# Experts' stage as one block: gates applied before the gather, scatters that add in DRAM, two buffers each for gathered rows, results and row numbers

## The chip, the core and the metric

One core of a Trainium2 chip runs the whole program as one launch. The metric is the time of that launch on the device in microseconds (us). The core has TensorE (PE, with its weight loads shown apart as PEld), VectorE (DVE), ScalarE (ACT), GpSimd (POOL), SyncE (SP), whose queue issues most DMAs, and 16 DMA engines that all queues share. POOL issues the indirect DMAs, whose row numbers come from a table.

## The reference, cut to what matters

The program is a two-layer decoder over x of 2 x 1024 tokens with 256 features: chunked attention, cross attention, a quantised feed-forward layer, causal attention, a second cross attention, and last a mixture of experts. Only this last stage, in which each token goes to 2 of 8 experts, is touched. From the kernel's view it is:

```python
xn = layernorm(x) * gamma + beta                 # 2048 tokens x 256
probs = clip(normalised_softmax(clip(xn @ router.T)), 1e-8, 1)
gates, expert = top_k(probs, 2)                  # 2 choices per token
for each choice i of token n:
    h = silu(W_gate[e] @ (gate * xn[n])) * (W_up[e] @ (gate * xn[n]))
    y[n, i] = W_down[e] @ h                      # e = expert[n, i], 512 hidden
out = layernorm(x + (x + y[n, 0] + y[n, 1]))     # so 2 x + the two results
```

## The kernel before, in words

Tokens are handled in 16 tiles of 128 (`TILES`). `stage_experts` (L2088) runs three blocks one after the other. A block is a piece of program for each engine with a barrier of all engines at its end.

The first block routes. It normalises x into `xn` (L2308 to L2231), writes it to DRAM as `xn_rows` (L2199), multiplies it by the router, and picks two experts and two gates per token (L2328 to L2336). Each of the 4096 choices gets a slot, counted expert by expert, each expert's slots padded to whole tiles of 128; that gives 39 slot tiles (`SLOT_TILES`). TensorE turns the table round, from "slot of a choice" to "choice and gate of a slot", by 32 matmuls of one-hot matrices (`at_place`, L2378) with `tile_values` (L2278) in fp32. The results are `token` (which row to gather), `choice` (which row to scatter to), `slot_gate` and `expert`, the expert of each slot tile.

The second block is the loop over the 39 slot tiles. `lagged` (L92) writes each engine's loop as a software pipeline: in step t an engine works on tile t and on tiles t-1 and t-2 (GpSimd down to t-4). Most of it is a hardware loop over four steps a turn, the rest is unrolled ahead and behind. For a tile:

- GpSimd copies a column of `token` into `tile_token` (L2425), gathers 128 rows from `xn_rows` (L2428), and multiplies them by the gate into `row` (L2420).
- TensorE transposes `row` (L2470). ScalarE rounds it to `rows_hi` (L2503), VectorE takes the remainder `rows_lo` (L2538). In the same way the expert's weights are split into `w_hi` (ScalarE, L2493) and `w_lo` (VectorE, L2528).
- TensorE does 12 matmuls for gate and up (L2463). ScalarE applies silu (L2498), VectorE multiplies into `hidden` (L2535). TensorE transposes it (L2453), VectorE copies that to `hidden_tr` (L2522), and TensorE does 4 down matmuls, shown as 8 rows (L2476).
- ScalarE copies the result to `rows_out` (L2508), the single buffer, which it may do only when the scatter of the tile before has landed (`need(act, scattered, 16 * u2)`). GpSimd copies a column of `choice` (L2433) and scatters 128 rows to `choice_rows` (L2436), in which each token has two rows.

The third block ends the stage: SP loads both rows of each token from `choice_rows` (L2602) in 8 groups of two tiles, GpSimd adds them (L2562), VectorE adds 2 x (L2575) and takes mean and variance (L2578 to L2584), GpSimd makes the scale and offset (L2554, L2557), ScalarE normalises (L2592), and SP writes the output (L2606).

Engines run their own instructions in the written order and wait only on semaphores. Four lines matter below: `pool.wait_ge(scattered, 16 * SLOT_TILES)` ends GpSimd's loop block (L2440), `need(act, scattered, 16 * u2)` is ScalarE's (L2507), `pe.wait_ge(row_ready, t + 1)` holds the transposes of rows for GpSimd (L2467), and `pe.wait_ge(hidden_ready, u2 + 1)` holds the transposes of hidden for VectorE (L2450).

## Time and profile before

| | |
|---|---|
| median of 3 runs | 1422.87 us (1421.18 to 1423.92) |
| the profiled execution | 1422.48 us, of which the span is 1420.8 us |
| experts' stage | about 1076 to 1420.8 us of the span |
| its loop, first transposes of rows to last scatter | 1150.8 to 1380.0 us |
| busy over the span | PE 84%, DVE 62%, ACT 52%, POOL 43% |
| mean granted TensorE clock | 0.929 of 2.4 GHz |

All times within the execution are counted from the start of the span. A row of the timeline gives start, duration, engine, source line, operation, what it writes and reads, how many were merged into the row, and in brackets how long the engine was idle before it and what released it. "<-issue" means that nothing in the profile released it. DMA rows on POOL or SPq are the issue; the transfer lands later. A row of a stretch gives busy time with the number of instructions in brackets, then the granted clock (1.00 is 2.4 GHz, 0.50 is 1.2 GHz).

### The profile page before, as it was taken

The numbers are of one execution on the slowest core, as the hardware profiler recorded it, in microseconds if no ns is written. First come the engines' busy times: TensorE is split into PE (matmuls) and PEld (weight loads), VectorE is DVE, ScalarE is ACT, GpSimd is POOL, SyncE is SP. The second block draws the span as 40 slices with busy tenths as digits, with TensorE's granted clock in tenths as the row PEclk, the third lists the DMA queues.
The fourth block names the chain that finished last, engine by engine and source line by source line (L and its number), as shares of the span: only waits on it lengthen the run. The fifth ranks groups of instructions, "written<-read, shape, count | busy, mean of one in ns | idle before, by whom it ended". The sixth has DMA issues, their size and how long they took to land. (4 is left out here: it accounts for less than half of the span.)

```text
span 1420.8 us, 25057 instructions
## 1 busy us (share of the span) xinstructions
PE 1197.0 (84%) x8059; PEld 873.5 (61%) x8060; DVE 881.0 (62%) x1545; ACT 743.3 (52%) x2046; POOL 608.3 (43%) x664
## 2 busy tenths in 40 slices
PE   7888589575999999999899999998984368999970
PEld 4544367454667767776666777665763357777750
DVE  2588799773445555563445566665886656677745
ACT  2598457334556556655555566652661035555532
POOL 1155457557436223322633322101664336666635
PEclk9999799797899999999999999999996569999995
DMA  9100000010010010001010001005401001111105
GB/s 303 27 1 0 0 1 2 1 30 16 16 30 16 16 30 16 16 1 31 15 25 17 5 16 45 1 1 224 133 1 45 23 19 49 44 48 48 48 33 178
DMA packets 36136, 56.04 MB, mean 39 GB/s; under 512 B 6528, under 2 KB 27392, under 8 KB 36032
## 3 DMA queue, kind: packets, MB, share of 16 engines
q1 hardware_dynamic: 32288, 44.47, 10.5%
q0 software_dynamic: 3744, 10.23, 2.2%
q8 instruction: 59, 0.97, 0.3%
q14 instruction: 45, 0.37, 0.1%
HBM read 34.90 MB, written 9.31 MB: 31 GB/s over the span
## 5 line engine op out<-in xcount | busy, mean ns | idle before, releaser
L2016 DVE TENSOR_REDUCE ga_neg_top<-ps 128x1 f32<-128x128 f32 (+7 forms) x256 | 181.9, 752 | 195.2 <-PE ps L1786 194.8
L1897 ACT ACTIVATE ga_e<-ps,ga_neg_top 128x128 f32<-128x128 f32 (+7 forms) x256 | 188.2, 743 | 7.5 <-DVE ga_neg_top L2016 6.8
L1906 ACT COPY ga_e_tr<-ps 128x512 f32<-128x512 f32 (+3 forms) x192 | 92.0, 479 | 174.6 <-PE ps L1795 172.1
L1795 PE MATMUL ps<-ident,ga_e 128*128 128x128 f32 x1152 | 165.1, 279 | 0.8 <-DVE ga_e_tr L2024 0.8
L1811 PE MATMUL ps<-ga_e_tr,ga_v 128*64 128x256 f32 x1152 | 151.7, 391 | 4.1 <-ACT ga_att L1914 4.1
L1795 PEld LDWEIGHTS ps<-ident,ga_e 128*128 128x128 f32 x1152 | 123.3, 142 | 28.0 <-ACT ga_e L1897 14.7
L2024 DVE COPY ga_e_tr<-ps 128x128 f32<-128x128 f32 (+3 forms) x192 | 105.8, 551 | 35.1 <-PE ps L1795 34.8
L2528 DVE TENSOR_TENSOR ex_w_lo<-ex_gate_up,ex_w_hi 128x1024 fp32r<-128x1024 f32 x78 | 92.7, 1229 | 42.1 <-ACT ex_w_hi L2493 42.0
L1971 POOL TENSOR_TENSOR ga_q_lo<-shared,ga_q_hi 128x1024 fp32r<-128x1024 f32 x15 | 35.5, 2370 | 175.5 <-ACT ga_q_hi L1887 175.5
L2493 ACT CAST ex_w_hi<-ex_gate_up 128x1024 fp32r x78 | 77.9, 1046 | 50.5 <-PEq L2189 35.0
L1811 PEld LDWEIGHTS ps<-ga_e_tr,ga_v 128*64 128x64 f32 x1152 | 72.4, 136 | 48.9 <-issue 23.3
L818 POOL TENSOR_TENSOR xa_e<-xa_e,xa_recip 128x1024 f32<-128x1024 f32 x32 | 60.9, 1902 | 68.6 <-DVE xa_recip L938 68.6
L1783 PE MATMUL ps<-ga_k_hi,ga_q_hi 64*128 64x512 f32 (+3 forms) x384 | 79.2, 409 | 4.1 <-PEq L158 2.3
L493 ACT ACTIVATE ca_e<-ps,ca_neg_top 128x64 f32<-128x64 f32 x256 | 75.9, 361 | 0.2 <-DVE ca_neg_top L524 0.2
L2476 PE MATMUL ps<-ex_down,shared 128*128 x312 | 74.0, 380 | 1.8 <-DVE shared L2522 1.0
L1957 POOL TENSOR_TENSOR shared<-shared,ga_cos 128x1024 f32<-128x1024 f32 x18 | 42.6, 2368 | 75.0 <-DMA shared<-shared 71.2
L2436 POOL DMA_INDIRECT choice_rows<-shared,ex_tile_choice x39 | 59.7, 1530 | 31.9 <-POOL ex_tile_choice L2433 31.9
L1247 PE MATMUL ps<-x_tr,wide_weights 128*128 128x128 f32 x512 | 67.0, 286 | 2.0 <-ACT ga_e_tr L1906 2.0
L1247 PEld LDWEIGHTS ps<-x_tr,wide_weights 128*128 128x128 f32 x512 | 62.9, 200 | 8.2 <-issue 5.8
L1783 PE MATMUL ps<-ga_k_lo,ga_q_hi 64*128 64x512 f32 (+3 forms) x384 | 67.6, 348 | 0.0
L1783 PE MATMUL ps<-ga_k_hi,ga_q_lo 64*128 64x512 f32 (+3 forms) x384 | 67.6, 348 | 0.0
L493 ACT ACTIVATION_READ_ACCUMULATOR ca_e<-ps,ca_neg_top 128x1 f32 x256 | 65.1, 255 | 0.0
(330 smaller groups left out, 2738.7 us busy)
## 6 DMA issues: line engine op xcount, KB each, us to landing
shared<-shared SPq DMA_DIRECT2D x80, 128.0 KB, 2.4
ex_gate_up<-in_ex_gate_up SPq DMA_DIRECT2D x1, 8192.0 KB, 24.3
ex_down<-in_ex_down SPq DMA_DIRECT2D x1, 4096.0 KB, 35.7
x_tr<-in_x_tr SPq DMA_DIRECT2D x4, 512.0 KB, 7.3
x_nat<-in_x SPq DMA_DIRECT2D x1, 2048.0 KB, 11.7
xn_rows<-x_tr SPq DMA_DIRECT2D x8, 256.0 KB, 2.1
x_tr<-choice_rows SPq DMA_DIRECT2D x8, 256.0 KB, 4.9
shared<-choice_rows SPq DMA_DIRECT2D x8, 256.0 KB, 5.5
```

The source lines that it names most:

```text
L493: last = nc.scalar.activation(e[buffer][:, keys], ps_scores[buffer][:, keys], ACT.Exp, scale=SCALE, bias=neg_top[buffer][:, m:m + 1], accu ...
L1247: last = nc.tensor.matmul(bank[:, g * P:(g + 1) * P], wq[:, k, block_of], x_tr[:, k, J * P:(J + 1) * P], start=(k == 0), stop=(k == KD - 1))
L1783: nc.tensor.matmul(ps_scores(t, half)[:, k0:k1], qs[J % 2][rows, c * R + r, :], ks[slot][rows, c, 0:k1 - k0], start=(i == 0), stop=(i == 2 ...
L1795: last = nc.tensor.transpose(ps_tr[n % 2][:, (kb - k0) * P:(kb - k0 + 1) * P], e[half][t % 2][:, kb * P:(kb + 1) * P], core.ident[:])
L1811: last = nc.tensor.matmul(ps_att[half * HD:(half + 1) * HD, :], v[:, v_slot(b, kb), kv * HD:(kv + 1) * HD], e_tr[g % 2][:, kb, half, :], s ...
L1897: nc.scalar.activation(e[half][t % 2][:, 0:blocks(t) * P], ps_scores(t, half), ACT.Exp, bias=neg_top[t % 2][:, half:half + 1], accum_out=s ...
L1906: nc.scalar.copy(e_tr[g % 2][:, k0:k1, half, t % 2 * P:(t % 2 + 1) * P], ps_tr[n % 2][:, 0:(k1 - k0) * P].rearrange("p (k t) -> p k t", t= ...
L2016: nc.vector.tensor_reduce(neg_top[t % 2][:, half:half + 1], ps_scores(t, half), AX.X, ALU.max, negate=True).then_inc(top_ready, 1)
L2024: nc.vector.tensor_copy(e_tr[g % 2][:, k0:k1, half, t % 2 * P:(t % 2 + 1) * P], ps_tr[n % 2][:, 0:(k1 - k0) * P].rearrange("p (k t) -> p k ...
L2476: last = nc.tensor.matmul(core.ps_y[:, 0:D], hidden_tr[:, k, :], weights.down[:, bass.ds(y, 1), k, :].rearrange("p a n -> p (a n)"), start ...
L2493: nc.scalar.copy(w_hi[turn % 2][:, k, :], weights.gate_up[:, bass.ds(x, 1), k, :] .rearrange("p a n -> p (a n)")).then_inc(w_hi_ready, 1)
L2528: nc.vector.tensor_tensor(w_lo[turn % 2][:, k, :], weights.gate_up[:, bass.ds(x, 1), k, :].rearrange("p a n -> p (a n)"), w_hi[turn % 2][: ...
```

## The change

The three blocks become one, so both barriers inside the stage go. Within it:

- ScalarE doubles x (4 instructions, L2399 of the new file) and SP writes it to DRAM as `summed_rows`, N + 128 rows. Each scatter then adds its rows there (`compute_op=ALU.add`) instead of writing `choice_rows`. Each scatter waits for the one before to have landed, since two choices of a token go to one row. Unused slots go to the 128 spare rows.
- The gates are applied ahead of the loop: ScalarE makes two scaled copies of `xn` (32 instructions, L2412) and SP writes both to `gated_rows` (16 DMAs of 256 KB). GpSimd's multiply in the loop goes, `xn_rows` goes too, and TensorE transposes the gathered rows themselves. The first gather and ScalarE's first step wait until all of it is written.
- With no gates to carry, the routing table has two parts of bf16 (tile number and place) instead of three of fp32. VectorE now makes both parts and both one-hot halves, running sums over the experts are 3 steps instead of 8, and both choices are handled in one instruction where there were two. The `past` and `expert` instructions move behind the one-hots.
- Gathered rows, `rows_out` and the row numbers for the scatter have two buffers each. A gather waits for the transposes of the tile two before and for the gather before it; ScalarE's copy waits for the scatter two before.
- The tail loads one tensor instead of two. GpSimd's adds and VectorE's 2 x + sum go. SP waits for the scatters itself. GpSimd executes an explicit drain behind its loop, ahead of the tail's work.

```diff
-        row, tokens_in, rows_out = (flat[:, i * D + 3 * FF:(i + 1) * D + 3 * FF] for i in (1, 2, 3))
+        rows_in, rows_out = ([flat[:, i * D + 3 * FF:(i + 1) * D + 3 * FF] for i in pair] for pair in ((1, 2), (3, 4)))
         hidden_tr = flat[:, D + 2 * FF:D + 3 * FF].rearrange("p (k t) -> p k t", k=KF)
...
-        choice_rows = nc.dram_tensor("choice_rows", (2 * N + P, D), F32).ap()
+        gated_rows = nc.dram_tensor("gated_rows", (2 * N, D), F32).ap()
+
+        summed_rows = nc.dram_tensor("summed_rows", (N + P, D), F32).ap()
...
+        def fetch(pool, g, turn):
+
+            nc.gpsimd.tensor_copy(tile_source[:], column(source, g)).then_inc(source_ready, 1)
+            pool.wait_ge(source_ready, g + 1)
+            apart(pool, core.pool_waited)
+            nc.gpsimd.indirect_dma_start(rows_in[turn % 2], None, gated_rows,
+                                         bass.IndirectOffsetOnAxis(ap=tile_source[:], axis=0)).then_inc(gathered, 16)
...
+                for n in range(TILES // DOUBLED):
+                    tiles = slice(n * DOUBLED, (n + 1) * DOUBLED)
+                    sp.wait_ge(doubled_ready, n + 1)
+                    sp.dma_start(summed_rows[0:N, :].rearrange("(n p) d -> p n d", p=P)[:, tiles, :],
+                                 doubled[n // len(HALVES)][:, HALVES[n % len(HALVES)], :]).then_inc(summed_written, 16)
+                sp.dma_start(summed_rows[N:N + P, :], doubled[0][:, 0, :]).then_inc(summed_written, 16)
+                for i in range(2):
+                    for g in range(GROUPS_OF_TILES):
+                        tiles = slice(g * GROUP, (g + 1) * GROUP)
+                        sp.wait_ge(gated_ready, i * GROUPS_OF_TILES + g + 1)
+                        sp.dma_start(gated_rows[i * N:(i + 1) * N, :].rearrange("(n p) d -> p n d", p=P)[:, tiles, :],
+                                     gated[i][:, tiles, :]).then_inc(gated_written, 16)
+
+                sp.wait_ge(scattered, 16 * SLOT_TILES)
                 for g in range(GROUPS_OF_TILES):
                     tiles = slice(g * GROUP, (g + 1) * GROUP)
-                    sp.wait_ge(xn_ready, g + 1)
-                    sp.dma_start(xn_rows.rearrange("(n p) d -> p n d", p=P)[:, tiles, :], xn[:, tiles, :]).then_inc(xn_written, 16)
-
-                sp.wait_ge(xn_written, 16 * GROUPS_OF_TILES)
+                    rows = summed_rows[0:N, :].rearrange("(n p) d -> p n d", p=P)
+                    sp.dma_start(xn[:, tiles, :], rows[:, tiles, :]).then_inc(sums_loaded[g], 16)
+                for g in range(GROUPS_OF_TILES):
+                    tiles = slice(g * GROUP, (g + 1) * GROUP)
+                    sp.wait_ge(final_ready, g + 1)
+                    sp.dma_start(core.out.rearrange("(n p) d -> p n d", p=P)[:, tiles, :], xn[:, tiles, :]).then_inc(out_written, 16)
+                sp.wait_ge(out_written, 16 * GROUPS_OF_TILES)
...
-                pool.wait_ge(masks_ready, MASKS)
-                pool.wait_ge(in_tile_ready, 1)
-                for i in range(2):
-                    for part, value in enumerate((choice_iota[:, i], gate_parts[:, 0, i])):
-                        nc.gpsimd.tensor_tensor(tile_values[:, i, :, part, :], in_tile[:, i], of_tiles(value), ALU.mult).then_inc(values_ready, 1)
+                pool.wait_ge(gated_written, 16 * 2 * GROUPS_OF_TILES)
+                pool.wait_ge(sources_ready, 1)
+                fetch(pool, 0, 0)
+
+                def step(g, t, u1, u2, u3, turn):
+                    if g is not None and not at(g, 0):
+                        need(pool, rows_tr_ready, g - 1)
+                        pool.wait_ge(gathered, 16 * g)
+                        apart(pool, core.pool_waited)
+                        fetch(pool, g, turn)
+                    if u3 is not None:
+                        pool.wait_ge(down_copied, u3 + 1)
+                        apart(pool, core.pool_waited)
+                        nc.gpsimd.tensor_copy(tile_target[turn % 2][:], column(target, u3)).then_inc(target_ready, 1)
+                        pool.wait_ge(target_ready, u3 + 1)
+                        need(pool, scattered, 16 * u3)
+                        apart(pool, core.pool_waited)
+                        nc.gpsimd.indirect_dma_start(summed_rows, bass.IndirectOffsetOnAxis(ap=tile_target[turn % 2][:], axis=0),
+                                                     rows_out[turn % 2], None, compute_op=ALU.add).then_inc(scattered, 16)
+
+                pool.wait_ge(targets_ready, 1)
+                pool.wait_ge(summed_written, 16 * (TILES // DOUBLED + 1))
+                lagged(pool, SLOT_TILES, 4, step, turns=True)
+                nc.gpsimd.drain()
+
+                def finish(g):
+                    tiles = slice(g * GROUP, (g + 1) * GROUP)
+                    pool.wait_ge(var_ready, g + 1)
+                    nc.gpsimd.tensor_tensor(rstd[:, tiles], var_eps[:, tiles], core.neg_half[:].to_broadcast([P, GROUP]),
+                                            ALU.pow).then_inc(rstd_ready, 1)
+                    pool.wait_ge(rstd_ready, g + 2)
+                    nc.gpsimd.tensor_tensor(offset[:, tiles], neg_mean[:, tiles], rstd[:, tiles], ALU.mult).then_inc(offset_ready, 1)
+
+                for g in range(GROUPS_OF_TILES):
+                    finish(g)
...
-                    for t in range(TILES):
-                        last = nc.tensor.matmul(ps_slots, at_place[:, t, :], tile_values[:, i, t, :, :],
-                                                start=(i == 0 and t == 0), stop=(i == 1 and t == TILES - 1))
-                    last.then_inc(slots_ready, 1)
+                    for n in range(i * TILES, (i + 1) * TILES):
+                        last = nc.tensor.matmul(ps_choice, at_place[:, n, :], choice_values[:, n, :, :], start=(n == 0), stop=(n == 2 * TILES - 1))
+                last.then_inc(slots_ready, 1)
...
+                    if t is not None:
+                        pe.wait_ge(gathered, 16 * (t + 1))
+                        need(pe, rows_lo_ready, t)
+                        for k in range(KD):
+                            last = nc.tensor.transpose(core.ps_q[:, k * P:(k + 1) * P], rows_in[turn % 2][:, k * P:(k + 1) * P], core.ident[:])
+                        last.then_inc(rows_tr_ready, 1)
...
+                act.wait_ge(core.x_loaded, 16)
+                for n in range(TILES // DOUBLED):
+                    tiles = slice(n * DOUBLED, (n + 1) * DOUBLED)
+                    nc.scalar.activation(doubled[n // len(HALVES)][:, HALVES[n % len(HALVES)], :], core.x_nat[:, tiles, :], ACT.Copy,
+                                         scale=2.0).then_inc(doubled_ready, 1)
...
+                act.wait_ge(xn_tr_ready, TILES // BATCHED)
+                for i in range(2):
+                    act.wait_ge(gates_ready, i + 1)
+                    for t in range(TILES):
+                        last = nc.scalar.activation(gated[i][:, t, :], xn[:, t, :], ACT.Copy, scale=gates[:, i, t:t + 1])
+                        if t % GROUP == GROUP - 1:
+                            last.then_inc(gated_ready, 1)
+
+                act.wait_ge(sources_ready, 1)
+                act.wait_ge(gated_written, 16 * 2 * GROUPS_OF_TILES)
+                act.wait_ge(summed_written, 16 * (TILES // DOUBLED + 1))
+                act.wait_ge(weights.loaded, 16 * weights.LOADS)
...
+                        need(act, scattered, 16 * (u2 - 1))
+                        nc.scalar.copy(rows_out[turn % 2], core.ps_y[:, 0:D]).then_inc(down_copied, 1)
...
+                for n, distance in enumerate((1, 2, 4)):
+                    summed = reach[n + 1][:, LEFT:] if n < 2 else ends[:]
+                    link(nc.vector.tensor_tensor(summed, reach[n][:, LEFT:], reach[n][:, LEFT - distance:LEFT - distance + EXPERTS], ALU.add))
+                link(nc.vector.tensor_tensor(starts[:], ends[:], count, ALU.subtract))
+
+                link(nc.vector.scalar_tensor_tensor(work[:], starts[:].unsqueeze(1).to_broadcast(by_tile), float(P), ps_rank[:, 0:TILES, :],
+                                                    ALU.mult, ALU.add))
+                link(nc.vector.tensor_tensor(picks[:], picks[:], work[:].unsqueeze(1).to_broadcast([P, 2, TILES, EXPERTS]), ALU.mult))
+                link(nc.vector.reduce_sum(slots_f[:], picks[:], AX.X))
...
+                one_hot(in_tile[:], tile_f[:].rearrange("p i t -> p (i t)"), slot_iota, SLOT_COLUMNS).then_inc(in_tile_ready, 1)
+                link(nc.vector.tensor_scalar(slots_part[:], slots[:], P - 1, None, ALU.bitwise_and))
+                link(nc.vector.tensor_copy(place_f[:], slots_part[:]))
+                dve.wait_ge(in_tile_ready, 1)
+                nc.vector.tensor_tensor(choice_values[:, :, 0, :], in_tile[:], of_tiles(tile_iota[:]), ALU.mult)
+                nc.vector.tensor_scalar(choice_values[:, :, 1, :], in_tile[:], place[:, 0:1], None, ALU.mult).then_inc(choice_values_ready, 1)
+                for i in range(2):
+                    one_hot(at_place[:, i * TILES:(i + 1) * TILES, :], place_f[:, i, :], place_iota, P).then_inc(places_ready, 1)
...
-                    dve.wait_ge(sum_ready, g + 1)
-
-                    link(nc.vector.scalar_tensor_tensor(core.x_nat[:, tiles, :], core.x_nat[:, tiles, :], 2.0, scratch[:, tiles, :],
-                                                        ALU.mult, ALU.add))
+                    dve.wait_ge(sums_loaded[g], 16)
                     for t in range(g * GROUP, (g + 1) * GROUP):
...
```

The loop steps of TensorE, ScalarE and VectorE are otherwise the same text, moved into the one block.

**Where instructions move.** GpSimd, one step inside the hardware loop before, where `shared` is the buffer that holds rows:

```order
L2420 REGISTER_ALU
L2420 TENSOR_TENSOR shared<-shared,ex_slot_gate 128x256
L2425 ISA
L2425 COPY ex_tile_token<-ex_token 128x1
L2426 REGISTER_ALU
L2428 DMA shared<-xn_rows,ex_tile_token 128x256
L2431 REGISTER_ALU
L2433 ISA
L2433 COPY ex_tile_choice<-ex_choice 128x1
L2436 DMA choice_rows<-shared,ex_tile_choice 4224x256
```

and the step after:

```order
L2285 REGISTER_ALU
L2199 ISA
L2199 COPY ex_tile_source<-ex_source 128x1
L2200 REGISTER_ALU
L2202 DMA shared<-gated_rows,ex_tile_source 128x256
L2289 REGISTER_ALU
L2291 ISA
L2291 COPY ex_tile_target<-ex_target 128x1
L64 REGISTER_ALU
L2295 DMA summed_rows<-shared,ex_tile_target 2176x256
```

The multiply L2420 is gone from the step; two copies and two indirect DMAs are left, and the second DMA now carries a wait for the one of the step before.

GpSimd, from the last scatter into the tail before, where the two branches are the end of one block and the start of the next:

```order
L2436 DMA choice_rows<-shared,ex_tile_choice 4224x256
L2406 UNCONDITIONAL_BRANCH
L2549 UNCONDITIONAL_BRANCH
L2562 TENSOR_TENSOR shared<-shared,x_tr 128x512 x2
L2554 TENSOR_TENSOR ex_rstd<-ex_var_eps,neg_half 128x2
L2557 TENSOR_TENSOR ex_offset<-ex_neg_mean,ex_rstd 128x2
L2562 TENSOR_TENSOR shared<-shared,x_tr 128x512
L2554 TENSOR_TENSOR ex_rstd<-ex_var_eps,neg_half 128x2
L2557 TENSOR_TENSOR ex_offset<-ex_neg_mean,ex_rstd 128x2
```

and after:

```order
L2295 DMA summed_rows<-shared,ex_tile_target 2176x256
L2306 TENSOR_TENSOR ex_rstd<-ex_var_eps,neg_half 128x2
L2309 TENSOR_TENSOR ex_offset<-ex_neg_mean,ex_rstd 128x2
L2306 TENSOR_TENSOR ex_rstd<-ex_var_eps,neg_half 128x2
L2309 TENSOR_TENSOR ex_offset<-ex_neg_mean,ex_rstd 128x2
L2306 TENSOR_TENSOR ex_rstd<-ex_var_eps,neg_half 128x2
```

The branches and the adds L2562 are gone; the drain is not listed, and stands between the first two rows.

VectorE, from the tile and place numbers to the one-hot matrices before (`ex_in_tile` and `ex_at_place`):

```order
L2371 CAST ex_gate_parts<-ex_gates 128x32
L2372 TENSOR_TENSOR ex_gate_parts<-ex_gates,ex_gate_parts 128x32
L2368 TENSOR_TENSOR ex_in_tile<-ex_tile_f,ex_slot_iota 128x640 x2
L2376 TENSOR_SCALAR ex_slots_part<-ex_slots 128x32
L2377 CAST ex_place_f<-ex_slots_part 128x32
L2368 TENSOR_TENSOR ex_at_place<-ex_place_f,ex_place_iota 128x2048
L2381 TENSOR_TENSOR ex_tile_values<-ex_in_tile,ex_gate_parts 128x16x40 x2
L2368 TENSOR_TENSOR ex_at_place<-ex_place_f,ex_place_iota 128x2048
```

and after:

```order
L2521 TENSOR_TENSOR ex_in_tile<-ex_tile_f,ex_slot_iota 128x1280
L2525 TENSOR_SCALAR ex_slots_part<-ex_slots 128x32
L2526 CAST ex_place_f<-ex_slots_part 128x32
L2528 TENSOR_TENSOR ex_choice_values<-ex_in_tile,ex_tile_iota 128x32x40
L2529 TENSOR_SCALAR ex_choice_values<-ex_in_tile,ex_place 128x32x40
L2521 TENSOR_TENSOR ex_at_place<-ex_place_f,ex_place_iota 128x2048 x2
```

Both one-hot halves now stand side by side, with a buffer each, where the second waited for TensorE to have read the first; and VectorE does the two products of `choice_values`, where GpSimd had done four of six.

## Rows read from the trace of the kernel before

**Rows 1.** Stretches: length, PE, PEld, DVE, ACT, POOL busy, PEclk, DMA share, GB/s
```profile
1240.00:1300.00 60.00, 57.84 (x282) 46.18 (x282) 42.85 (x55) 34.55 (x55) 39.51 (x55) 1.00 0.15 48
1397.00:1400.00 3.00, 0.00 (x0) 0.00 (x0) 2.90 (x8) 1.09 (x2) 2.67 (x5) 0.50 1.09 357
```

**Rows 2.** Timeline, GpSimd, one turn of the loop; start, us, what, idle before
```profile
1247.02 1.01 POOL L2428 DMA_INDIRECT shared<-xn_rows,ex_tile_token  x1 [0.80 <-ACT shared L2508]
1248.03 0.20 POOL L2433 COPY ex_tile_choice<-ex_choice 128x1 int32 x1
1249.05 1.51 POOL L2436 DMA_INDIRECT choice_rows<-shared,ex_tile_choice  x1 [0.82 <-POOL ex_tile_choice L2433]
1250.58 0.70 POOL L2420 TENSOR_TENSOR shared<-shared,ex_slot_gate 128x256 f32<-128x256 f32 x1
```

**Rows 3.** Timeline, TensorE and ScalarE, the same turn
```profile
1245.98 0.66 PE L2453 MATMUL ps<-ident,shared 128*128 128x128 f32 x4
...
1249.44 1.89 PE L2476 MATMUL ps<-ex_down,shared 128*128 x8
...
1251.46 0.43 PEld L2453 LDWEIGHTS ps<-ident,shared 128*128 128x128 f32 x4 [0.53 <-DVE shared L2535]
...
1252.03 0.37 ACT L2508 COPY shared<-ps 128x256 f32<-128x256 f32 x1 [2.01 <-DMA choice_rows<-shared,ex_tile_choice]
```

**Rows 4.** The scatters of line 2436: duration of an issue, and landing
```profile
L2436 POOL DMA_INDIRECT choice_rows<-shared,ex_tile_choice x39: 978/1533/1836, 1170.8 to 1379.0; - x39
...
DMA to landing us min/median/max: 2.4/3.0/3.3
```

**Rows 5.** Landing of the gathers of line 2428
```profile
DMA to landing us min/median/max: 2.6/2.8/3.5
```

**Rows 6.** Timeline, third and last transposes of hidden, and the first wait
```profile
1169.50 0.66 PE L2453 MATMUL ps<-ident,shared 128*128 128x128 f32 x4
...
1173.25 0.37 ACT L2508 COPY shared<-ps 128x256 f32<-128x256 f32 x1 [5.21 <-DMA choice_rows<-shared,ex_tile_choice]
...
1373.25 0.60 PE L2453 MATMUL ps<-ident,shared 128*128 128x128 f32 x4
```

**Rows 7.** Timeline, from the gates to the first transposes of rows
```profile
1112.94 0.29 DVE L2328 TENSOR_REDUCE ex_gates<-ex_probs 128x16 f32<-128x128 f32 x1
...
1118.17 0.17 DVE L2339 TENSOR_SCALAR ex_count<-ps 128x8 f32<-128x8 f32 x1 [1.38 <-PE ps L2269]
...
1137.69 2.29 DVE L2368 TENSOR_TENSOR ex_at_place<-ex_place_f,ex_place_iota 128x2048 fp32r<-128x2048 f32 x1 [3.83 <-PE ps L2278]
...
1145.73 0.18 POOL L2425 COPY ex_tile_token<-ex_token 128x1 int32<-128x1 int32 x1 [10.75 <-SPq L2406]
...
1146.85 1.23 POOL L2428 DMA_INDIRECT shared<-xn_rows,ex_tile_token  x1 [0.93 <-POOL ex_tile_token L2425]
...
1150.84 0.66 PE L2470 MATMUL ps<-ident,shared 128*128 128x128 f32 x2 [7.14 <-POOL shared L2420]
```

**Rows 8.** DMA issues of the page: count, size, median us to landing
```profile
xn_rows<-x_tr SPq DMA_DIRECT2D x8, 256.0 KB, 2.1
```

**Rows 9.** Timeline, from the last scatter to the last normalisation
```profile
1378.97 0.98 POOL L2436 DMA_INDIRECT choice_rows<-shared,ex_tile_choice  x1 [0.79 <-POOL ex_tile_choice L2433]
1388.27 0.36 SPq L2602 DMA_DIRECT2D x_tr<-choice_rows  x1
...
1392.21 1.26 POOL L2562 TENSOR_TENSOR shared<-shared,x_tr 128x512 f32<-128x512 f32 x1 [12.25 <-DMA shared<-choice_rows]
...
1397.36 1.09 ACT L2592 ACTIVATE x_tr<-x_nat,ex_offset,ex_rstd 128x256 f32<-128x256 f32 x2 [19.53 <-POOL ex_offset L2557]
...
1413.20 0.75 DVE L2578 BATCH_NORM_STATS2 ex_stats<-x_nat 128x6 f32<-128x256 f32 x2
...
1414.35 0.16 DVE L2584 TENSOR_SCALAR ex_var_eps<-ex_mv 128x2 f32<-128x2 f32 x1
...
1415.59 1.09 ACT L2592 ACTIVATE x_tr<-x_nat,ex_offset,ex_rstd 128x256 f32<-128x256 f32 x2 [0.46 <-POOL ex_offset L2557]
```

321 lines of the change are left out of this document (116 added, 205 removed).

## The prediction

> **What bounds the kernel now.** I read in this order: the busy shares by stage, the timeline of one turn of the experts' loop, the landing times of its two indirect DMAs, and then what stands ahead of the loop and behind it. Everything before 1076 us is the same program, so only the stage counts.
>
> In the middle of the loop TensorE is busy 57.8 of 60 us at a granted clock of 1.00 [rows 1]. The loop is thus close to what TensorE itself needs, and not quite there. One step runs from the transposes of hidden at 1245.98 to the next at 1251.46, 5.48 us. TensorE's own work in it ends with the down matmuls at 1249.44 + 1.89 = 1251.33, so it needs 5.35 and then waits for VectorE's hidden [rows 3]. Behind that stands ScalarE's copy of the result, which could start at 1251.4 and starts at 1252.03, released by the scatter; the splitting of weights for the next step follows it. The scatter is late since GpSimd has no gap: gather issue 1.01, copy 0.20, a launch of 0.82, scatter issue 1.51, multiply until 1251.28, together 4.26 us, and the copy and launch of the next gather fill the remaining 1.22 [rows 2]. So GpSimd's chain sets the step, with TensorE 0.13 us behind it.
>
> Over the whole loop this is worse than in the clean step. From the third transposes of hidden (tile 2, 1169.50) to the last (tile 38, 1373.25) there are 36 steps in 203.75 us, 5.66 each [rows 6]. The excess is the first scatter, for which ScalarE waits 5.21 us [rows 6], and a longer step at each of the turns of four.
>
> Ahead of the loop the path is VectorE's: ranks at 1118.17, the second one-hot half only at 1137.69, since it reuses a buffer that TensorE must have read, then TensorE, the barrier, and GpSimd's first copy at 1145.73 [rows 7]. Behind it nothing runs from the last scatter's issue (1378.97 + 0.98) to SP's first load at 1388.27, though a scatter lands 2.4 to 3.3 us after its start [rows 4, 9]. Then VectorE and GpSimd take turns until 1415.59.
>
> **Ahead of the loop: 12.7 us less.** After the ranks VectorE has 13 small instructions (0.17 us [rows 7] and about 0.04 between, 2.7 together), three of 128 to 256 columns (an estimate of 1.2), and three of 1280 and two of 2048 columns. The 2048 took 2.29 undisturbed [rows 7], 1.12 ns a column, so 7936 columns are 8.9. I take no faster rate for bf16, which would give 1 us. The last one-hot ends at 1118.17 + 12.8 = 1131.0. The moved expert instructions (1280 columns in all of 320 and 40, about 1.4) hide TensorE's last matmuls. Five small ones give the source rows at 1133.5.
>
> The gated copies run beside this. ScalarE was idle here. Gates of choice 0 exist at 1113.2, 32 activations at 1.09 / 2 = 0.545 each [rows 7, 9] make 17.4, so the last is at 1130.7; with an issue of 0.36 and a landing of 2.1 [rows 8, 9] all is written at 1133.2. That is 256 KB in 1.09 us, 240 GB/s, where the tail moved 357 [rows 1]. The doubled rows are written while ScalarE and the DMAs have little to do, 1076 to 1090, and cost nothing; were they late, they would stand only before the first scatter.
>
> GpSimd then copies (1.12 to the gather's start, as at 1145.73 to 1146.85) and gathers. Start 1134.7, landing 2.6 to 3.5 [rows 5, 7], I take 3.3 for a first one; TensorE transposes at 1138.1, with no multiply between. Before it was 1150.84 [rows 7]: 12.7. Bounds: 10 if the writes land 3 us later, 14 if bf16 is fast.
>
> **The loop: 11.2 us less.** The multiply (0.70 [rows 2]) leaves GpSimd. Left are 0.18 + 0.80 + 1.01 + 0.20 + 0.82 + 1.51 = 4.5 [rows 2, 7], under TensorE's 5.35. ScalarE's copy now needs the scatter two before, so it starts 0.6 earlier and the chain to hidden with it, and TensorE wanted only 0.13. The next that is late is TensorE itself: 36 steps at 5.35 are 192.6, 11.2 less. Between 5.25 (the modelled ends of its matmuls overlap the next by 0.1) and 5.45 (turns of four still cost) it is 15 to 8. The first two steps I leave.
>
> Two costs the trace does not show. The issue of an adding scatter: between the plain 1.53 and twice that, 3.1, as it names each row to read and to write [rows 4]; I take near 1.53. GpSimd has 0.85 us of room. Its landing: between the plain 3.0 [rows 4] and 3.0 + 2.8 = 5.8, a scatter after a whole gather [rows 4, 5]. I take 3.6, as most of a landing is fixed time that one read ahead of the write should not double. The new wait puts a scatter at least landing + 0.82 after the one before; it binds from a landing of 4.5. Behind it in GpSimd's queue stands the next gather, which has over a step of lead.
>
> The trace has 0.98 us for a scatter's issue while VectorE is idle [rows 9] and 1.51 in the loop [rows 2]. The Trainium skill (SBUF — State Buffer, SBUF: two separate sides) says that an instruction of VectorE that holds the ports it shares with GpSimd keeps GpSimd from writing descriptors. By that rule a gather moved under the weight splits would also grow by some 0.5 us, and the step's sum would be 5.0 instead of 4.5; that alone would not make GpSimd the bound.
>
> **From the last transposes to the loads: 6.3 us less.** Before, 1373.25 to 1388.27 is 15.0 [rows 6, 9]. Now the down matmuls, the copy and the launch put the last scatter at + 5.6 or so (it was + 5.72), it lands 3.1 later in a quiet queue, and SP waits for that itself: 8.7.
>
> **The tail: 11.3 us less.** Before, 27.3 from first load to the last group at ScalarE. Two loads landed 3.9 after the first issue; one is there after about 3.4. Of the VectorE step remain 1.31 (1413.20 to 1414.35 + 0.16), GpSimd's and ScalarE's parts of a group are shorter (ScalarE 1.09). So 3.4 + 7 x 1.31 + 2.4 (1413.20 to 1415.59) = 15.0 [rows 9]. The drain may take as long as the silence before 1388.27, which would hold GpSimd some 1 to 2 us past the first variance, and it catches up; I add 1.0. Writing the output is unchanged.
>
> **Sum.** 12.7 + 11.2 + 6.3 + 11.3 = 41.5 off 1422.48, the profiled execution (1420.8 of span and 1.7 around it; the median is 0.4 more): 1381 us.
>
> **Rivals.**
> - GpSimd stays the bound, as adding scatters take longer to issue. For it: it has no gap now, and a launch costs 0.8 even for nothing. Against: 0.85 of room. From an issue of 2.4 it decides; at a step of 5.66 the loop gives nothing and the time is 1392, at 3.1 (step 6.1) it is 1407.
> - The scatters' own chain becomes the bound and the kernel is slower. 39 adding scatters follow each other, each landing + 0.82. At the upper bound of 5.8 the step is 6.6, 36 x 1.27 = 46 more than forecast, and two such landings at the end make 50: 1431. It breaks even from 5.6; between 4.5 and 5.6 the time lies from 1383 to 1422. For it: read, add and write of the same row in one transfer. Against: 128 rows lie over 16 engines, 8 each, and a plain scatter needs only 1.5 us behind its issue [rows 2, 4].
> - The gated writes are late: 4 MB on one queue. If each needed its 2.1 alone the last would land at 1148 and the time were 1395. Against: the rate of 357 GB/s with several in flight [rows 1].
>
> On the second of these the Trainium skill (DMA: Bandwidth & Descriptors, Two DMAs through the same engine are not ordered) reports that of two read-modify-write packets on one queue the second often read stale data when it directly followed. They overlap, then, which speaks for a landing near the lower bound; no run so far shows it here.
>
> **Chances.** The forecast with 1374 to 1388 has 0.58, GpSimd as the bound 0.17, landings between 4.5 and 5.6 0.10, slower by landings 0.07, late writes 0.05, 0.03 for what I don't see. The range is 1374 (front 14, loop 15, no drain cost) to 1404, with half of the middle landings outside. 0.2% is about what a measurement can tell from no change. Faster 0.90, same 0.02, slower 0.08.
>
> **What would show it.** First transposes of rows near 1138; steps of 5.35 with no idle of TensorE before the transposes of hidden; ScalarE's copy released by the down matmuls; landing of the adding scatter under 4.5; SP's first load some 9 us behind the last transposes of hidden; groups of the tail 1.3 apart. Wrong would make it: GpSimd without gaps, GpSimd waiting for a scatter before each scatter, or the first gather held by the writes.

## The result, and the profile of the changed kernel

The changed kernel takes 1377.23 us (median of 4 runs, 1375.69 to 1378.32) against 1422.03 of the kernel before: a ratio of 0.9684 with a 95% interval of 0.9666 to 0.9701, 44.8 us less. The forecast was 1381. The profiled execution has a span of 1376.4 us, 44.4 less than before. Below, the terms are measured between the spans.

The loop first, in the view of stretches (length, then the busy time of each engine, TensorE's granted clock, DMA share, GB/s):

```profile
1240.00:1300.00 60.00, 59.41 (x296) 48.53 (x296) 45.23 (x58) 35.94 (x57) 40.98 (x46) 1.00 0.29 48
```

TensorE is busy 59.4 of 60 us, where it was 57.8 [rows 1]. The DMA share has doubled at the same 48 GB/s: the adding scatters read as well as write (with scatters that only write, experiment 1, it is 0.16 at 50 GB/s). Next the timeline of one turn on GpSimd, then ScalarE's, VectorE's and TensorE's in the same stretch:

```profile
1244.42 1.67 POOL L2295 DMA_INDIRECT summed_rows<-shared,ex_tile_target  x1 [0.89 <-PE ps L2381]
1245.53 0.76 POOL L2199 COPY ex_tile_source<-ex_source 128x1 int32 x1
1247.08 1.01 POOL L2202 DMA_INDIRECT shared<-gated_rows,ex_tile_source  x1 [0.79 <-POOL ex_tile_source L2199]
1248.09 0.96 POOL L2291 COPY ex_tile_target<-ex_target 128x1 int32 x1
1249.95 1.67 POOL L2295 DMA_INDIRECT summed_rows<-shared,ex_tile_target  x1 [0.89 <-POOL ex_tile_target L2291]
...
1247.79 2.36 DVE L2566 TENSOR_TENSOR ex_w_lo<-ex_gate_up,ex_w_hi 128x1024 fp32r<-128x1024 f32 x2 [0.73 <-ACT ex_w_hi L2426]
...
1245.86 0.37 ACT L2441 COPY shared<-ps 128x256 f32<-128x256 f32 x1 [1.44 <-PE ps L2387]
...
1245.58 0.60 PE L2364 MATMUL ps<-ident,shared 128*128 128x128 f32 x4
...
1250.80 0.66 PE L2364 MATMUL ps<-ident,shared 128*128 128x128 f32 x4
```

Against rows 2 and 3: the multiply is gone, ScalarE's copy is released by the down matmuls and no more by the scatter, and TensorE's step is 5.22 instead of 5.48. But GpSimd has no gap here either. This turn of it takes 5.53, the one before took 4.89, and the difference is the copy of the target's row number: 0.96 here, 0.32 there. It starts at 1248.09 beside VectorE's first split (1247.79, half of 2.36) and ends at 1249.05, just behind it. The other copy, 0.76 at 1245.53, is no such case: its row starts while the scatter's issue still runs, to 1246.09, and it ends 0.20 behind that. Starts of TensorE's transposes of hidden are three times 5.22 and once 5.57 apart; from the third (1155.36) to the last (1345.93) there are 36 steps in 190.6 us, 5.29 each, against 203.75 [rows 6].

The scatters by their line (issue, min/median/max ns; what held them; landing), against rows 4:

```profile
L2295 POOL DMA_INDIRECT summed_rows<-shared,ex_tile_target x39: 1557/1667/2152, 1154.5 to 1353.6; - x39
...
  DMA summed_rows<-shared,ex_tile_target: 10.5, 4
...
DMA to landing us min/median/max: 3.5/3.9/4.4
```

The page's chain that ended last, by engine, shares of the span:

```profile
POOL 7%; issue 6%; DMA 3%; POOLq 1%; DVE 1%; SPq 0%; ACT 0%; ACTq 0%; DVEq 0%
```

No TensorE is in it: in the loop this chain runs through GpSimd's copies, launches and issues. It can't show that a copy was held up by VectorE, so it doesn't say alone what sets the step; experiment 1 helps with that.

Ahead of the loop and behind it, timeline:

```profile
1118.17 0.17 DVE L2501 TENSOR_SCALAR ex_ends<-ps 128x8 f32<-128x8 f32 x1 [1.38 <-PE ps L2344]
...
1124.91 0.55 DVE L2529 TENSOR_SCALAR ex_choice_values<-ex_in_tile,ex_place 128x1280 bf16<-128x1280 bf16 x1
1125.38 4.49 DVE L2521 TENSOR_TENSOR ex_at_place<-ex_place_f,ex_place_iota 128x2048 bf16<-128x2048 f32 x2
...
1133.71 1.24 POOL L2202 DMA_INDIRECT shared<-gated_rows,ex_tile_source  x1 [0.94 <-POOL ex_tile_source L2199]
...
1136.89 0.66 PE L2381 MATMUL ps<-ident,shared 128*128 128x128 f32 x2 [5.73 <-DMA shared<-gated_rows,ex_tile_source]
...
1345.93 0.60 PE L2364 MATMUL ps<-ident,shared 128*128 128x128 f32 x4
...
1349.01 1.57 POOL L2295 DMA_INDIRECT summed_rows<-shared,ex_tile_target  x1 [2.15 <-DMA summed_rows<-shared,ex_tile_target]
...
1349.58 0.37 ACT L2441 COPY shared<-ps 128x256 f32<-128x256 f32 x1 [3.08 <-PE ps L2387]
...
1353.59 1.56 POOL L2295 DMA_INDIRECT summed_rows<-shared,ex_tile_target  x1 [2.81 <-DMA summed_rows<-shared,ex_tile_target]
1361.69 0.73 POOL L2306 TENSOR_TENSOR ex_rstd<-ex_var_eps,neg_half 128x2 f32<-128x2 f32 x1 [6.55 <-DVE ex_var_eps L2592]
...
1357.29 3.94 SPq L2239 DMA_DIRECT2D x_tr<-summed_rows  x8
...
1368.68 0.74 DVE L2586 BATCH_NORM_STATS2 ex_stats<-x_tr 128x6 f32<-128x256 f32 x2
```

First transposes of rows at 1136.89, before 1150.84 [rows 7]. The last scatter could have followed its rows (copied at 1349.95) by 1.1 and starts 3.6 behind them, since it waits for the landing of the one before. It lands at 1357.28 and SP's first load stands 11.4 behind the last transposes, where it was 15.0 [rows 6, 9]. From there to the last start of statistics it is 11.4 us, before 24.9 [rows 9].

| term | predicted | measured | how |
|---|---|---|---|
| ahead of the loop | 12.7 | 14.0 | 1150.84 to 1136.89 |
| first transposes of rows to last of hidden | 11.2 | 13.4 | 222.4 to 209.0 |
| to SP's first load | 6.3 | 3.7 | 15.0 to 11.4 |
| tail | 11.3 | 13.4 | 1420.8 - 1388.27 to 1376.4 - 1357.29 |

### The profile page after: what moved, and what is told of

The parts are those of the page before. It is cut to its first block and busy times, and to the rows that moved or that the text cites. A ratio compares the mean times of both kernels' runs of the same rounds, so it can differ in the third digit from the quotient of the medians.

```text
span 1376.4 us, 24979 instructions
## 1 busy us (share of the span) xinstructions
PE 1186.4 (86%) x8059; PEld 868.3 (63%) x8060; DVE 865.8 (63%) x1528; ACT 763.2 (55%) x2082; POOL 586.3 (43%) x616
## 3 DMA queue, kind: packets, MB, share of 16 engines
q1 hardware_dynamic: 34544, 46.70, 11.3%
q0 software_dynamic: 7488, 10.23, 4.6%
## 5 line engine op out<-in xcount | busy, mean ns | idle before, releaser
L2295 POOL DMA_INDIRECT summed_rows<-shared,ex_tile_target x39 | 65.4, 1676 | 41.6 <-PE ps L2381 16.0
```

What stands on the lines that cost most here:

```text
L2295: nc.gpsimd.indirect_dma_start(summed_rows, bass.IndirectOffsetOnAxis(ap=tile_target[turn % 2][:], axis=0), rows_out[turn % 2], None, comp ...
```

## The experiments

All are timed against the kernel before; "the changed kernel" is 1377.2 us. "Loop" is the first to the last start of the transposes of hidden as the views by line give them, 201.5 us in the changed kernel and 214.8 before.

**1. Writing instead of adding.**

```diff
-    rows_out[turn % 2], None, compute_op=ALU.add).then_inc(scattered, 16)
+    rows_out[turn % 2], None).then_inc(scattered, 16)
```

> The scatters write instead of adding; the sum over the two choices is left out. Theory A (TensorE sets the step of the loop; adding costs landing time, which is seen only at the end, where the last four scatters follow each other by landing + 0.8): issue of a scatter back from 1.67 to about 1.53, landing from 3.9 to 3.0, the loop unchanged at 5.29 a step, SP's first load about 2 to 3 us earlier: 1374 to 1376. Theory B (GpSimd's chain of two launches and an adding scatter still sets the step with TensorE): 0.14 less for each of 38 steps and the end besides: 1369 to 1371.

1373.87 us (ratio 0.9657, 0.9639 to 0.9675). The scatters by line, the last of them on the timeline, a stretch of the loop, and the chain of the page:

```profile
L2295 POOL DMA_INDIRECT summed_rows<-shared,ex_tile_target x39: 988/1001/2002, 1153.6 to 1350.2; - x39
...
1350.22 0.99 POOL L2295 DMA_INDIRECT summed_rows<-shared,ex_tile_target  x1 [0.82 <-POOL ex_tile_target L2291]
1357.76 0.73 POOL L2306 TENSOR_TENSOR ex_rstd<-ex_var_eps,neg_half 128x2 f32<-128x2 f32 x1 [6.55 <-DVE ex_var_eps L2592]
...
1240.00:1300.00 60.00, 59.48 (x297) 48.75 (x296) 44.53 (x56) 36.47 (x57) 35.90 (x47) 1.00 0.16 50
...
PE 11%; DVE 4%; issue 3%; DMA 2%; POOL 1%; ACT 1%; ACTq 0%; POOLq 0%; DVEq 0%
```

The issue falls by 0.67, more than expected, and the loop stays at 201.4: theory A. GpSimd is busy 35.9 of 60 us instead of 41.0 and waits for TensorE in two turns of four (0.70 and 0.96), the chain now runs through TensorE, and TensorE's steps are still three times 5.22 and once 5.57. So a full GpSimd is not what keeps the loop at this length. The last scatter follows its rows by 1.1 and lands within 2.5 (SP's first load at 1352.7); the end is 3.7 shorter. So adding costs nothing in the loop and 3.7 at the end: 2.5 for the wait on the landing before, 1.2 for the last landing.

**2. One buffer for results.**

```diff
-    rows_out[turn % 2], None, compute_op=ALU.add).then_inc(scattered, 16)
+    rows_out[0], None, compute_op=ALU.add).then_inc(scattered, 16)
...
-    need(act, scattered, 16 * (u2 - 1))
-    nc.scalar.copy(rows_out[turn % 2], core.ps_y[:, 0:D]).then_inc(down_copied, 1)
+    need(act, scattered, 16 * u2)
+    nc.scalar.copy(rows_out[0], core.ps_y[:, 0:D]).then_inc(down_copied, 1)
```

> One result buffer instead of two, and ScalarE's copy waits for the scatter before. Theory A (the second buffer is what takes ScalarE off the scatter): an adding scatter frees its buffer 3.9 us after its start, later than a plain one, so ScalarE's copy is released by the scatter again and the split of weights behind it starts late; the chain from copy to launch (0.3 + 0.8), landing (3.9) and the next copy (0.5) is 5.5 or more against 5.29: 36 x 0.3 = 11 us more or beyond, 1388 to 1400. Theory B (the multiply that left GpSimd is what gave the gain; the buffer is idle detail): within 2 us of 1377.

1390.96 us (0.9780, 0.9761 to 0.9799). What ScalarE's copy was held by in all:

```profile
L2441 ACT COPY shared<-ps x39: 372/372/375, 1148.2 to 1363.5; 128x256 f32<-128x256 f32 x39
...
  DMA summed_rows<-shared,ex_tile_target: 81.1, 38
```

The loop is 214.9, the length of before: with one buffer an adding scatter takes back the whole gain of the loop. Theory A. One buffer with a scatter that only writes was not run.

**3 and 4. One and two multiplies more on GpSimd**, behind each scatter, whose results nobody reads.

```diff
+    need(pool, pad_ready, PADS * u3)
...
+    for buffer in padded:
+        nc.gpsimd.tensor_tensor(buffer, core.x_nat[:, 0, :],
+            column(starts, 0).to_broadcast([P, D]), ALU.mult).then_inc(pad_ready, 1)
```

> GpSimd gets one more multiply of 128x256 in each step (0.70 us), behind the scatter, whose result nobody reads. The change had taken such a one away. Theory A (GpSimd's room under TensorE's step is the 0.85 of the prediction): within 2 us of 1377. Theory A' (its records: 4.89 from one scatter to the next where it waits for nothing but its own launches, so 0.3 to 0.4 of room): 36 x 0.35 = 12 more, 1387 to 1391. Theory B (GpSimd has no room and sets the step): 38 x 0.70 = 27 more, 1404.

1408.84 us (0.9897, 0.9877 to 0.9918).

> As the one before, with two such multiplies (1.40 us a step). Theory A: 1.40 - 0.85 = 0.55 a step, 20 more, 1397. Theory A': 1.40 - 0.35 = 1.05 a step, 38 to 40 more, 1416. Theory B: 1.40 a step, 53 more, 1430. From the difference of this run and the one before, the full price of 0.70 on GpSimd once it is the bound: 25 to 27 us by A' and B.

1425.70 us (1.0025, 1.0015 to 1.0034). One turn of GpSimd with one multiply (experiment 3):

```profile
1242.14 2.11 POOL L2298 DMA_INDIRECT summed_rows<-shared,ex_tile_target  x1 [1.01 <-issue]
1243.72 1.18 POOL L2303 TENSOR_TENSOR shared<-x_nat,ex_starts 128x256 f32<-128x256 f32 x1
1244.32 0.70 POOL L2201 COPY ex_tile_source<-ex_source 128x1 int32 x1
1245.82 1.02 POOL L2204 DMA_INDIRECT shared<-gated_rows,ex_tile_source  x1 [0.80 <-POOL ex_tile_source L2201]
...
1247.94 1.60 POOL L2298 DMA_INDIRECT summed_rows<-shared,ex_tile_target  x1 [0.90 <-POOL ex_tile_target L2294]
```

In experiment 3 the loop is 230.4, 0.76 more a step, for an instruction of which 0.65 stick out behind the scatter. GpSimd had no room at all, so A and A' are wrong and B is nearest, with 31.6 us where it said 27. The second multiply (experiment 4) adds only 16.9, 0.43 a step, which no theory had. More work on GpSimd also moves what falls beside VectorE's split; whether that makes the second one cheaper is not shown. Experiment 10 looks at the other sign.

**5. The scatter one turn earlier in GpSimd's order.**

```diff
-    lagged(pool, SLOT_TILES, 4, step, turns=True)
+    lagged(pool, SLOT_TILES, 3, step, turns=True)
```

The buffer numbers of the scatter are moved by one to match.

> GpSimd issues the scatter of a tile one turn earlier in its order (it runs three tiles behind the gather, not four). Theory A (the last four scatters follow each other by landing + 0.8 because they are one turn late; with an earlier turn each waits for its own copied result only): loop as before, the last scatter starts about 2.5 us earlier, 1373 to 1376. Theory B (GpSimd then waits for the copied result ahead of each gather, and the gathers come too late for TensorE): TensorE waits for the gather in most steps, 0.3 to 0.6 a step, 1388 to 1400.

1381.09 us (0.9713, 0.9692 to 0.9733). TensorE's transposes of rows, what held them:

```profile
L2381 PE MATMUL ps<-ident,shared x78: 270/273/448, 1137.8 to 1343.8; 128*128 128x128 f32 x78
...
  DMA shared<-gated_rows,ex_tile_source: 17.8, 29
```

Both happen. The end is 1.0 shorter (10.0 against 11.0), not 2.5, and the gathers come late, so the loop is 205.6, 4.1 longer. B has the sign, at a quarter of its price.

**6. The tail in a block of its own.**

```diff
-    nc.gpsimd.drain()
...
+    pool.wait_ge(scattered, 16 * SLOT_TILES)
...
+        with nc.Block() as block:
```

The new block holds the loads, statistics, powers, normalisation and stores.

> The tail stands in a block of its own again; GpSimd waits for the last scatter at the end of the first block, and everything else is as in the changed kernel. Theory A (GpSimd's end of a block is silent for some 8 us counted from its last indirect DMA, as 1379.96 to 1388.27 of the kernel before): the last scatter's issue ends at about 1355.2, so the loads start at 1363.5 instead of 1357.3, 6 us more: 1383. Theory B (only a barrier between engines, under 2 us, counted from the landing): 1378 to 1379. Theory C (the silence starts at the landing, 1357.3 + 8): 1385.

1383.97 us (0.9732, 0.9711 to 0.9753).

```profile
1353.06 1.56 POOL L2285 DMA_INDIRECT summed_rows<-shared,ex_tile_target  x1 [2.44 <-DMA summed_rows<-shared,ex_tile_target]
...
1363.70 1.39 SPq L2598 DMA_DIRECT2D x_tr<-summed_rows  x3
```

The last transposes of hidden to the first load take 17.1 instead of 11.0. The time is that of theory A, its way of counting is not: from the issue's end to the load it is 9.1 here and 8.3 in the kernel before [rows 9]. Counted from the landing it is 6.9 here, if this one took the 3.7 of the changed kernel's last. So GpSimd waits for the landing, and then some 7 us follow. Experiments 1 and 8 show what they are.

**7. The kernel before with two buffers for results**, a second one for the target's row numbers, and a wait of each scatter for the one before.

```diff
-    need(act, scattered, 16 * u2)
-    nc.scalar.copy(rows_out, core.ps_y[:, 0:D]).then_inc(down_copied, 1)
+    need(act, scattered, 16 * (u2 - 1))
+    nc.scalar.copy(rows_out[turn % 2], core.ps_y[:, 0:D]).then_inc(down_copied, 1)
```

> The kernel before with two buffers for results and for scatter rows, nothing else; the multiply stays on GpSimd. Theory A (without the multiply gone GpSimd has no gap, so the buffer gives only the stall of 5.2 us at the first scatter or less): 1416 to 1422. Theory B (the buffer alone takes the wait off ScalarE and gives the loop's gain): 1409 to 1412. Together with the run with one result buffer this tells whether each of the two edits works alone or only both.

1434.77 us (1.0096, 1.0075 to 1.0117): slower than before by 14, which neither theory had. One turn:

```profile
1247.00 1.01 POOL L2429 DMA_INDIRECT shared<-xn_rows,ex_tile_token  x1 [0.79 <-POOL ex_tile_token L2426]
1248.02 0.20 POOL L2434 COPY ex_tile_choice<-ex_choice 128x1 int32 x1
1249.23 1.02 POOL L2438 DMA_INDIRECT choice_rows<-shared,ex_tile_choice  x1 [1.02 <-issue]
1250.27 0.81 POOL L2421 TENSOR_TENSOR shared<-shared,ex_slot_gate 128x256 f32<-128x256 f32 x1
1251.31 0.89 POOL L2426 COPY ex_tile_token<-ex_token 128x1 int32 x1 [0.24 <-POOL shared L2421]
...
1249.38 2.77 DVE L2530 TENSOR_TENSOR ex_w_lo<-ex_gate_up,ex_w_hi 128x1024 fp32r<-128x1024 f32 x2 [0.72 <-ACT ex_w_hi L2495]
...
1251.13 0.44 PE L2472 MATMUL ps<-ident,shared 128*128 128x128 f32 x2 [0.59 <-POOL shared L2421]
```

Against rows 2 the scatter's issue is shorter (1.02 for 1.51), but the multiply and the copy of a row number, 0.70 and 0.19 before, now lie beside VectorE's split and take 1.00 and 0.87 on average. GpSimd's gapless step is 6.0, and TensorE waits for its rows. VectorE's two halves of the split are held up too, 2.77 for 2.36. In the kernel before, the wait of ScalarE for the scatter had also tied the split to the scatter:

```profile
1248.45 2.36 DVE L2528 TENSOR_TENSOR ex_w_lo<-ex_gate_up,ex_w_hi 128x1024 fp32r<-128x1024 f32 x2 [0.94 <-ACT ex_w_hi L2493]
```

Beside it lay the scatter's issue (1249.05 to 1250.56) and only 0.2 of the multiply. Theory B's gain did not come there: the buffer cost 14.

**8. No drain.**

```diff
-    nc.gpsimd.drain()
```

> The changed kernel without GpSimd's drain behind the loop. Theory A (the drain is over before the first variance of the tail is there, since GpSimd waited 6.5 us for VectorE then): within 2 us of 1377. Theory B (the drain or what it waits for still delays GpSimd's first power): 1 to 3 us less.

1381.03 us (0.9714, 0.9694 to 0.9734): 3.8 more, against both theories. GpSimd's last scatter, its first power and its last:

```profile
1353.38 1.56 POOL L2295 DMA_INDIRECT summed_rows<-shared,ex_tile_target  x1 [2.31 <-DMA summed_rows<-shared,ex_tile_target]
1361.23 0.73 POOL L2305 TENSOR_TENSOR ex_rstd<-ex_var_eps,neg_half 128x2 f32<-128x2 f32 x1 [6.29 <-DVE ex_var_eps L2591]
...
1370.46 0.19 POOL L2308 TENSOR_TENSOR ex_offset<-ex_neg_mean,ex_rstd 128x2 f32<-128x2 f32 x1
```

The first power now follows VectorE at once. But the program ends 8.3 us behind GpSimd's last instruction (1370.65 to 1379.0), where in the changed kernel it ends 5.4 behind it (1371.04 to 1376.4). This fits a drain that is done at the end of the block in any case, and that lies beside loads and statistics when it is put behind the loop; no record shows the one at the end itself. Its length can be read in two kernels: the first power starts 6.54 behind the last scatter's issue in the changed kernel (1355.15 to 1361.69) and 6.55 in experiment 1 (1351.21 to 1357.76), whatever VectorE did: its first variance was there 0.37 before the power in the one and 1.00 before it in the other. From first load to end it is 21.9 us against 19.1. The loop, which the edit does not touch, is 202.8, with an issue of 2.25 in the median: another pattern of GpSimd and VectorE, 1.3 us dearer, in which the scatter's issue lies beside the split and waits for the landing before it in 25 of 38 turns. Experiments 4, 5, 6 and 10 show issues of 2.24 to 2.30 too.

**9. The second one-hot half waits for TensorE again.**

```diff
+    need(dve, slots_ready, i)
-    one_hot(at_place[:, i * TILES:(i + 1) * TILES, :], place_f[:, i, :], place_iota, P)
+    one_hot(at_place[:, 0:TILES, :], place_f[:, i, :], place_iota, P)
```

> The second half of the one-hot rows of the routing stands in the buffer of the first again, so VectorE waits for TensorE between the halves as it did before the change; the rest of the new front stays. Theory A (most of the 14 us ahead of the loop come from the independence of the halves and from what is no longer behind the second one): TensorE needs about 16 x 0.1 to 0.2 us for a half, and VectorE waits for it once, 2 to 4 us: 1379 to 1381. Theory B (the gain is of the smaller number of small VectorE instructions and of the barrier; the halves overlap anyway): within 1 us of 1377.

1377.47 us (0.9685, 0.9669 to 0.9701). VectorE waits 1.41 and the first transposes of rows come at 1138.5, 1.6 later; the time does not show it beyond what it can tell, which is theory B's time, and the loop is 201.2. The halves' independence is thus 1.6 of the 14.0 at most; the rest should be what no longer stands on the path (the multiply, the barrier, values for each half), which no run took apart.

**10. GpSimd copies both row numbers in one instruction.**

```diff
-    nc.gpsimd.tensor_copy(tile_source[:], column(source, g)).then_inc(source_ready, 1)
+    both = pairs[:, g, :] if isinstance(g, int) else pairs[:, bass.ds(g, 1), :].rearrange("p a n -> p (a n)")
+    nc.gpsimd.tensor_copy(tile_pair[turn % 2][:], both).then_inc(source_ready, 1)
...
-    nc.gpsimd.tensor_copy(tile_target[turn % 2][:], column(target, u3)).then_inc(target_ready, 1)
```

> The changed kernel, but the row numbers to gather and to add to stand side by side in one table, so that GpSimd copies them in one instruction a step instead of two. Theory A (TensorE is the bound of the changed loop, GpSimd has a little room): the loop keeps its 201.5 us or loses at most 3 (TensorE's idle time in it is 12.7 in all, most of it in the first steps), 1374 to 1377. Theory B (GpSimd still sets the step at many places): 0.3 to 0.7 less of GpSimd's work a step, 10 or more us less, 1367 or under.

1377.54 us (0.9683, 0.9666 to 0.9700), loop 202.2. A stretch of it, and the scatters:

```profile
1240.00:1300.00 60.00, 59.66 (x295) 48.24 (x294) 45.56 (x58) 35.63 (x56) 40.13 (x35) 1.00 0.30 48
...
L2302 POOL DMA_INDIRECT summed_rows<-shared,ex_tile_pair x39: 1557/2297/2617, 1153.7 to 1354.2; - x39
```

The time is theory A's, but the run does not decide between the two: GpSimd hardly gets less to do. The scatter's issue grows from 1.67 to 2.30, so that it is busy 40.1 of 60 us against 41.0 with a copy fewer each turn. What decides is experiment 1, where 5.1 us in 60 really are gone and the loop keeps its length. With experiment 3 this says that GpSimd and the chain of TensorE, ScalarE and VectorE are even at 5.29: more on GpSimd costs, less gives nothing.

**11. As 7, with VectorE's split cut to 8 columns.**

```diff
-    nc.vector.tensor_tensor(w_lo[turn % 2][:, k, :], ...
+    nc.vector.tensor_tensor(w_lo[turn % 2][:, k, 0:8], ...
```

> The kernel before with two result buffers, and VectorE's split of the weights cut from 1024 to 8 columns an instruction (the low part of the weights is left out but for these). Theory A (in the run with two result buffers in the kernel before, GpSimd's multiply and its copy fell beside VectorE's split and took 1.00 and 0.87 us instead of 0.70 and 0.19; that made its gapless step 6.0): with VectorE idle there they are back at 0.70 and 0.19, the step is TensorE's 5.2 to 5.3, and the loop 29 us shorter: 1404 to 1410. Theory B (GpSimd's times depend on something else, such as the two indirect DMAs in flight together): the step stays at 6.0 and the time at 1430 to 1435.

1403.26 us (0.9865, 0.9849 to 0.9882). GpSimd in the loop, and a stretch of it:

```profile
L2421 POOL TENSOR_TENSOR shared<-shared,ex_slot_gate 128x256 f32<-128x256 f32 x35 | 21.9, 625 | 3.6 <-issue 1.7 <-PE ps L2472 0.6 <-DMA shared<-xn_rows,ex_tile_token 0.5
...
L2426 POOL COPY ex_tile_token<-ex_token 128x1 int32 (+1 forms) x34 | 6.3, 185 | 7.9 <-POOL shared L2421 7.9
...
1240.00:1300.00 60.00, 60.00 (x306) 50.55 (x305) 23.94 (x59) 36.69 (x59) 35.75 (x59) 1.00 0.16 52
```

Theory A, and a little beyond it: multiply and copy are back at 0.63 and 0.19, the loop is 196.0 instead of 228.6 (32.6 less, where 29 were expected), TensorE has no gap, and its step is 5.16.

**12. ScalarE casts the next tile's weights ahead of its copy of the result**, while it waits for the down matmuls.

```diff
-def step(t, u1, u2, turn):
-    if t is not None:
-        x = expert_at(act, t)
-        need(act, gate_up_ready, t - 1)
...
+def step(w, t, u1, u2, turn):
...
+    if w is not None:
+        x = expert_at(act, w)
+        need(act, gate_up_ready, w - 1)
...
-lagged(act, SLOT_TILES, 2, step, turns=True)
+lagged(act, SLOT_TILES, 3, step, turns=True)
```

Here w is t + 1. Behind each `need` stand the casts into `w_hi`; the second place is behind silu and the cast of the rows, ahead of the copy of the result.

> The changed kernel, with ScalarE's casts of the weights of the next tile ahead of its copy of the result, in the 1.5 us for which it waits for the down matmuls; the copy of the result comes up to 0.6 later. Theory A (TensorE's last idle time in the loop, some 0.15 a step, is the wait for VectorE's hidden, which stands behind a split that waits for ScalarE's casts; without it the step is the 5.16 of the run without the split): up to 5.5 us less in the loop, 1372 to 1375. Theory B (VectorE's split moves to an earlier place in the step, where GpSimd's issues and copies then fall beside it, and the scatters' order of landing + 0.8 does the rest): GpSimd's step goes over 5.3, and the time is 1380 or more.

1372.65 us (median of 5 runs, 1371.55 to 1373.38; 0.9646, 0.9633 to 0.9659): faster than both kernels.

```profile
1240.00:1300.00 60.00, 60.00 (x306) 50.25 (x304) 46.70 (x59) 37.47 (x59) 40.36 (x48) 1.00 0.30 50
...
1243.84 0.37 ACT L2441 COPY shared<-ps 128x256 f32<-128x256 f32 x1
```

TensorE is busy in every part of the stretch with VectorE's full work beside it. The loop is 196.5, 5.0 less, each step 5.14 to 5.19, and the long fourth step is gone although the turns of four are still there. Theory A. GpSimd has no gap here either; its copy of the target's row number takes 0.61 on average instead of 0.75 (1160 to 1340), so it got shorter by as much as a step did. That the gain starts with ScalarE's order and not with that copy is concluded from the edit and from experiment 1, where the long fourth step stood with GpSimd waiting.

## Why the prediction was right

**Ahead of the loop.** 14.0 for 12.7. The one-hot halves cost what was taken (4.49 for two), but one of the two multiplications by a value is a tensor_scalar on bf16, 0.55 us for 1280 columns where 1.43 was in the sum. The gather also started 1 us earlier than taken (1133.71 for 1134.7). The gated copies were never near the path: 16 in 6.5 us, 0.405 each instead of 0.545, all written some 5 us ahead of the gather. The third rival did not come true.

**The loop.** 13.4 for 11.2: the step came to 5.29 for 5.35, and the first scatter's stall, 5.21 before [rows 6], is gone whole. That ScalarE comes off the scatter and the multiply off GpSimd was right: experiment 2 shows that without the second buffer the loop is as long as before (with adding scatters), experiment 7 that the second buffer without the multiply's removal makes it longer. That TensorE is "the next that is late", with 5.35 of its own, was not: experiments 11 and 12 show that it can do a step in 5.16, and at 5.29 it waits in part for the chain through ScalarE and VectorE and stands even with GpSimd. The sign "no idle of TensorE before the transposes of hidden" held nearly (busy 59.4 of 60 us).

**GpSimd's room.** Here a step of the working failed: "GpSimd has 0.85 us of room", from a sum of 4.5 against 5.35. Experiment 3 found none, and "GpSimd without gaps", a sign of being wrong, is in the trace. The sum had taken the copies at 0.2 and the scatter's issue at 1.51; in the turns above it is 4.89 and 5.53, since the copy beside the split takes 0.32 and 0.96 and the adding issue 1.67. The first rival was thus closer than the chance of 0.17 said: the two bounds met, and a further 0.7 would have cost 32 us. That the other chain was at 5.29 as well was luck. The 0.5 that the prediction feared for a gather under the splits exists where the issue starts second: the one at 1146.51, 0.05 behind a split, takes 2.02. In the middle of the loop the gather starts first (1242.19 against 1242.26) and stays at 1.01.

**Landing.** 3.9 for 3.6, under the 4.5 from which it binds in the loop, and the loop keeps its length when the adding goes (experiment 1). The rival on the slower side was wrong in its price, 5.8. The Trainium skill (DMA: Bandwidth & Descriptors, Two DMAs through the same engine are not ordered) says that the descriptors of one queue start in order but overlap. A landing that adding makes 0.9 longer, and not 2.8, agrees; no run here shows the overlap itself.

**To the loads.** 3.7 for 6.3, the term that was mis-sized. "the last scatter at + 5.6" let it follow its rows; it came at + 7.7, behind the landing of the one before. The wait was named in the prediction as one that binds only above 4.5, but GpSimd enters the end a whole step late and each scatter can make up only the step less landing and launch. The lateness is not all of it: with the scatter a turn earlier (experiment 5) the last one still waited 2.3 us for a landing. Experiment 1 prices the wait: 2.5, and 1.2 for the landing.

**The tail.** 13.4 for 11.3. The first load is there after 2.7, not 3.4, and groups are 1.21 apart, not 1.31. The drain was put at 1.0; it costs 0.3 (the first power 0.37 behind VectorE, not 0.09), and without it 2.8 would be paid at the end (experiment 8).

The errors, + 1.3, + 2.2, - 2.6 and + 2.1, make 3 us, since they partly cancel: that the sum is nearer than its terms is luck.

## What to carry to other kernels

Where an engine has no gap, taking a wait off another engine may only move what falls beside what: tie the two edits together and look at which instructions of GpSimd then lie under VectorE's. Before a change to a loop, look for an engine that waits while work for the next turn is already possible, as ScalarE did here for 1.4 us a turn; this gave 5 us of the loop, where 0.67 us a turn less on GpSimd (experiment 1) gave none. A chain of dependent transfers that is hidden in the loop is paid at its end, where each waits for the landing before it, so work out the last ones apart.
